# First gather stage of a graph network kernel: eight slots for gathered rows in place of four

## The reference, cut to what matters

```python
h = jnp.maximum(_layernorm(x, axis=-1), 0.0)
x_i = x[dst]
x_j = x[src]
edge_features = jnp.concatenate([x_i, x_j - x_i], axis=-1)
h = jax.nn.relu(edge_features @ W1 + b1)
edge_messages = h @ W2 + b2
out = jax.ops.segment_max(edge_messages, dst, num_segments=x.shape[0])
```

## Time and profile before

| | before |
|---|---|
| median of 3 runs | 5961.24 us (5958.34 to 5966.22) |
| span of the profiled execution, first to last instruction | 5916.2 us |
| instructions | 34006 |
| POOL busy | 3570.2 us (60%) |
| PE busy | 2544.0 us (43%) |
| DVE busy | 2042.2 us (35%) |
| ACT busy | 1398.4 us (24%) |

### The profile page before, as it was taken

How to read it: one execution, slowest core, us unless ns; L and a number is a source line. 1 busy time by engine, 2 the same in 40 slices (tenths; PEclk the granted TensorE clock), 3 DMA queues, 4 the chain that set the end, 5 groups by cost and what they waited for, 6 DMA issues and landing times. The chain is left out here.

```text
span 5916.2 us, 34006 instructions
## 1 busy us (share of the span) xinstructions
PE 2544.0 (43%) x8675; PEld 1514.2 (26%) x8675; DVE 2042.2 (35%) x2739; ACT 1398.4 (24%) x2486; POOL 3570.2 (60%) x3776
## 2 busy tenths in 40 slices
PE   2114444444444444441144444443444444457776
PEld 1012222222222222221022222222222222235555
DVE  5212222222222222224322222222222222269995
ACT  6101111111111111111111111111111111148884
POOL 5666666666666666665566666666666666631112
PEclk9986655666566666665565566566666656668887
DMA  9512222222222222222233333333333333369993
GB/s 356 161 44 66 73 70 68 72 70 70 69 70 74 66 73 71 68 72 50 53 95 91 87 97 87 98 98 87 97 88 98 88 93 93 96 211 420 422 420 130
DMA packets 351133, 696.87 MB, mean 118 GB/s; under 512 B 133445, under 2 KB 190543, under 8 KB 304247
## 3 DMA queue, kind: packets, MB, share of 16 engines
q1 hardware_dynamic: 204908, 558.27, 25.6%
q0 software_dynamic: 119328, 128.91, 10.9%
q10 hardware_dynamic: 26706, 7.50, 0.6%
HBM read 349.70 MB, written 344.74 MB: 117 GB/s over the span
## 5 line engine op out<-in xcount | busy, mean ns | idle before, releaser
L985 POOL DMA_INDIRECT pairs<-norm_table,node_sums x1664 | 1573.8, 946 | 795.7 <-issue 473.4
L711 POOL DMA_INDIRECT send_in<-send_table,node_sums x1664 | 1573.8, 946 | 773.0 <-issue 486.2
L1006 PE MATMUL ps_hid<-pairs_t,w1a 128*128 128x512 f32 x832 | 689.6, 924 | 1146.5 <-issue 667.8
L723 PE MATMUL ps_msg<-hidden,w_twice 128*128 128x512 f32 x416 | 423.0, 1119 | 1338.3 <-issue 919.3
L1095 DVE TENSOR_SCALAR hid<-ps_hid,vec 128x512 f32<-128x512 f32 x416 | 311.7, 749 | 1743.8 <-remote 989.0
L1041 ACT COPY pairs_t<-ps_pairs 128x512 f32<-128x512 f32 x416 | 244.0, 587 | 1640.1 <-DMA recv_edges<-node_sums 1100.7
L794 DVE TENSOR_TENSOR_SCAN filled<-mask,filled,ps_recv 128x512 f32<-128x512 f32 x208 | 266.2, 1280 | 879.9 <-ACT mask L757 712.4
L757 ACT COPY mask<-ps_mask 128x512 f32<-128x512 f32 x208 | 121.9, 586 | 1652.3 <-remote 894.2
L1228 DVE TENSOR_TENSOR_SCAN total<-ps_mask,total,hid 128x1024 f32<-128x1024 f32 x208 | 488.7, 2350 | 49.7 <-PE ps_mask L1178 24.8
L1006 PEld LDWEIGHTS ps_hid<-pairs_t,w1a 128*128 128x128 f32 x832 | 182.8, 273 | 1232.5 <-issue 721.1
L785 DVE TENSOR_TENSOR_SCAN maxima<-mask,maxima,ps_msg 128x512 f32<-128x512 f32 x208 | 266.2, 1280 | 631.7 <-issue 347.3
(11 more groups left out here) (174 smaller groups left out, 2952.9 us busy)
## 6 DMA issues: line engine op xcount, KB each, us to landing
hid_edges<-hid SPq DMA_DIRECT2D x104, 1024.0 KB
hid<-hid_edges SPq DMA_DIRECT2D x104, 1024.0 KB
hid_edges<-rows SPq DMA_DIRECT2D x104, 1024.0 KB
recv_edges<-node_sums SPq DMA_DIRECT2D x52, 1024.0 KB
recv_in<-recv_edges SPq DMA_DIRECT2D x208, 256.0 KB
max_edges<-max_rows SPq DMA_DIRECT2D x208, 256.0 KB
edge_in<-in_edge_attr_dram SPq DMA_DIRECT2D x415, 128.0 KB
send_in<-send_table,node_sums POOLq DMA_INDIRECT x1664
```

The lines of the kernel that those rows point to most:

```text
L711: pool.indirect_dma_start(out=send_in[:, s, j, t, :], out_offset=None, in_=send_table, in_offset=bass.IndirectOffsetOnAxis(ap=src_cols[:, ...
L723: nc.tensor.matmul(ps_msg[:, :], w2_twice[:, :], hidden[:, s % 2, :], start=True, stop=True).then_inc(msg_done, 1)
L985: pool.indirect_dma_start(out=pairs[:, s, j, 0:C], out_offset=None, in_=norm_table, in_offset=bass.IndirectOffsetOnAxis(ap=src_cols[:, k, ...
L1006: nc.tensor.matmul(ps_hid[s % 2][:, :], w1a[:, :], pairs_t[:, s % 2, :], start=True, stop=True).then_inc(multiplied, 1)
```

## The change

`send_in` gets eight slots, and each slot its own semaphore in `gathered`. POOL's step k waits until PE has turned step k-8 instead of step k-4, and PE waits for the semaphore of slot k modulo 8. `U`, by which the other buffers go, stays at four.

```diff
             U = 4
...
-            send_in = tensor(s2, "send_in", [P, U, J, 2, C])
+            DEEP = 8
+            send_in = tensor(s2, "send_in", [P, DEEP, J, 2, C])
...
-            gathered = [sem(f"gathered{i}") for i in range(U)]
+            gathered = [sem(f"gathered{i}") for i in range(DEEP)]
...
                 def gather(r, s):
                     k = r * U + s
-                    at_least_apart(pool, send_turned, k - U + 1, pool_passed)
+                    at_least_apart(pool, send_turned, k - DEEP + 1, pool_passed)
                     for t in range(2):
                         for j in range(J):
-                            pool.indirect_dma_start(out=send_in[:, s, j, t, :], out_offset=None, in_=send_table,
+                            pool.indirect_dma_start(out=send_in[:, k % DEEP, j, t, :], out_offset=None, in_=send_table,
                                                     in_offset=bass.IndirectOffsetOnAxis(ap=src_cols[:, t * HB + k, j:j + 1], axis=0)
-                                                    ).then_inc(gathered[s], 16)
+                                                    ).then_inc(gathered[k % DEEP], 16)
...
-                    at_least(pe, gathered[s], 16 * 2 * J * (r + 1))
+                    at_least(pe, gathered[k % DEEP], 16 * 2 * J * (k // DEEP + 1))
                     at_least(pe, join_done, k - 1)
                     for j in range(J):
-                        mm = nc.tensor.transpose(ps_send[s % 2][:, j::J], send_in[:, s, j, :, :].rearrange("p t c -> p (t c)"), ident[:, :])
+                        mm = nc.tensor.transpose(ps_send[s % 2][:, j::J], send_in[:, k % DEEP, j, :, :].rearrange("p t c -> p (t c)"), ident[:, :])
```

## The result

| | before | after |
|---|---|---|
| median of the runs, us | 5962.91 (5958.34 to 5966.22, 4 runs) | 5995.01 (5988.67 to 6004.24, 4 runs) |
| ratio | 1 | 1.0055, 95% interval 1.0044 to 1.0067 |
| profiled execution: span, us | 5916.2 | 5996.8 |

The account below looks back on a forecast made before the run. PE, held back by POOL's unbroken gathers, was taken as the bound. POOL ending 5.8 us earlier and PE's +30.3 at the end gave +24.5: 5916.2 + 45.0 + 24.5 = 5986 us, range 5944 to 6000 (own range 5973 to 6000).

Parts of the forecast that it names:

- Slots and semaphores cost nothing: Eight slots and semaphores add no instruction cost; POOL issues the same 1664 gathers: estimate 0.
- The middle keeps its pace: First gather stage, middle: the run-and-pause pattern shifts by four steps, pace stays 11.290 us a step, change 0.
- First wait before step 12, twelve steps of gathers against four joins: Stage's beginning: POOL first waits at step 12; at 464 us twelve steps of gathers stand against four joins.
- Its length, 9.0 us: POOL's first wait lasts 9.0 us, so step 12 starts at 473.7; bounds 4.1 and 15.5 us.
- Four more steps of PE at the end, +30.3 us: Stage's end: PE is at step 199, not 203, and does four more steps alone at 7.58 us: +30.3.
- POOL done a few us earlier: Stage's end: POOL's step 207 starts at 2675.3 against 2681.07, 5.8 us earlier.
- 45.0 us lie around the span: Profiled span 5916.2 us is 45.0 below the runs' median 5961.24; these 45.0 were taken as lying around the span.
- The reading that unbroken gathers hold PE back: First gather stage: long unbroken runs of POOL's gathers hold PE back, and a pause of POOL frees it.
- no change: Rival, chance 0.23: PE's late results have another cause, such as its own instruction count; 5961 us.
- A little faster: Rival, chance 0.10: the crawl of steps 2 and 3 belongs to the start itself; -14.8 us, 5946 us.
- Far faster: Rival, chance 0.07: POOL's pauses are the trouble and vanish; -232 us, 5729 us.
- Much slower: Rival, chance 0.05: runs of seven steps replace three, 12.9 us a step, +300 us, above 6200 us.

Follow-up runs that it names:

- the other trace of before: The unchanged kernel with four slots, profiled once more on another chip: 5981.01 us, span 5979.3 us.
- the runs without gathers: Kernel before with each step's eight gathers replaced by plain loads of other rows: 5115.67 us issued by SP, 5131.21 us by POOL.
- the gathers that nobody waits for: Kernel before with PE working on SP's plain loads, POOL issuing its 1664 gathers into tiles nobody reads: 7032.2 us (before 5954.48).

## Why the prediction was right, and where it was off

- **Slots and semaphores cost nothing**: right. Eight slots at the old distance, 0.9996.
- **The middle keeps its pace**: right. 158 joins in 1800 us in the changed and in the unchanged kernel, 157 with two and with sixteen slots. The absolute mark, 11.290 us a step, was too narrow: between the 41st and the 191st join the trace of after has 11.41, two executions of before 11.27 and 11.44. The reason given, one pattern shifted by four steps, was not tested by itself; what stays open, below, names another. The same holds for "some 70 waits": 101 after, 110 in an unchanged kernel.
- **First wait before step 12, twelve steps of gathers against four joins**: right (96 gathers, 4 joins).
- **Its length, 9.0 us**: the term that was mis-sized. It is 15.17 us, and I had the right value as the upper bound (15.5, if the wait grows with the run). In these traces it does: 5.6, 9.3, 15.2 and 26.2 us with 2, 4, 8 and 16 slots. So POOL's step 12 starts 1.7 us later than before from the stage's start, not 4 us earlier. My bound for a step held throughout, 40.6 us, was near the 42.0 that it is; with it, step 4 is turned at 478 and the wait is 13 us (478 - 464.7).
- **Four more steps of PE at the end, +30.3 us**: right. +30.5 us between the two traces, 26.6 against the other trace of before in the table.
- **POOL done a few us earlier**: not between these two traces, where its last step starts 2357.0 us after its first gather against 2336.6 before. The middle of after is slower in that execution, and so is its second stage; against the 2363.1 of the other trace of before, it is 6 us earlier.
- **The sum**: 1.7 + 30.5 + 0 for the middle = 32.2 us, and the medians differ by 32.1. I had 24.5, with -4.1 for step 12 and -1.8 that came in by 11.290 us a step, where the same trace has 11.299 from step 12 on. That the parts meet the medians within 0.1 us is partly luck: each varies by some us from trace to trace.
- **"45.0 us lie around the span"**: wrong. Each run's time is 1.9 us above its own span (5998.66 against 5996.8 in the profiled run of after). The profiled execution of before was itself shorter: 5918.1 us by this, with 5958.34 the shortest of the timed ones. On other chips the kernel before has medians of 5919 and 5925 us, so the trace may be of another chip. The forecast was not hurt, since the 24.5 us were added to the median in effect.
- **The reading that unbroken gathers hold PE back**: shown. PE at 42.0 us a step beside gathers with which it shares nothing, at 7.5 us once they are over. **That a pause frees it** was too simple. Pauses of 1.8 us free nothing, and the longer the run, the later PE comes free: POOL's last gather ended 9.4 us before the held join in before (414.27 to 423.63), 14.9 in after (470.5 to 485.45) and 26.0 with sixteen slots (578.6 to 604.55), after some 70, 120 and 230 us of gathers. Where they ran for 2303 us (to 2653), the join at 2672.07 still came 42.0 us after the one before it, and the next followed after 10.5.
- **The second gather stage as support**: weaker than it was put. Of its 5.65 us a step, four gathers alone take 5.0 by the 10.02 us for eight.

The rivals: *no change* falls with the runs without gathers (PE's own instruction count allows 7.5 us a step) and with sixteen slots. *A little faster* falls with 42.0 us, step after step, far from the stage's start. *Far faster* falls with sixteen slots, where gathers issued twelve steps earlier cost 1.36%, and with the gathers that nobody waits for, which took 2303 us and not 2085. The Trainium skill's rule (issue early, wait late: "DMA: Bandwidth & Descriptors", rules for kernel authors) did not help here: PE had waited 13.0 us for gathered rows. *Much slower* falls with the unchanged middle.

What stays open: by what path a gather holds PE back; whether it is its indirect form or its 128 single rows (no plain load of single rows was tried); and why the middle settles near 11.4 us a step, with anything from two to sixteen slots and with eight more PE instructions.

To the last question one answer fits the numbers; it was not tested: gathers, in the long run, do not go faster than one in 1.40 us. As an estimate from the run in which nobody waits for them, eight are then 11.2 us; the second gather stage has 5.65 us for four, 1.41 each. POOL issues one in 1.25 us for as long as a run is short, and what is left over after 70, 120 and 230 us of it, a share of 0.15 / 1.40, would be 7.5, 12.9 and 24.6 us, near the 9.4, 14.9 and 26.0 us above. If so, POOL's waits in the middle are time that it could not have used in any case. A run of gathers with PE at rest would tell.

## What to carry to other kernels

Before deepening a buffer, look at who is late: where the consumer is, the filler stands exactly as many steps ahead as there are slots, and every further slot only adds a step to what is left after the filler's last one (7.5 us here). Its waits are then not idle time to be won, however large their sum; the fewest slots that keep the consumer fed are best, two here (one was not tried). And a slow consumer may be slowed by the filler itself: give it the same data by another way, or run the filler for nobody, and see. The second also tells how fast the filler is without its waits: 2303 us here, against 2345 with them.

## What the runs showed of the hardware that was not expected

- While POOL issues gathers without a pause, PE gets through one weight load or product in 1.400 us: 42.0 us for a step of 30, 53.20 us for one of 38, and 42.00 us at either level of its clock. Without gathers the step of 30 takes 7.5 us.
- 3328 plain loads of 32 KB, issued by POOL with 0.3 us of idle time, and 167 GB/s in all, did nothing to PE.
- Where SP issued eight plain loads a step beside them, and POOL waited for nobody, gathers came 1.25 us apart for the first 200 us or so and 1.40 us later, as many as the loads and products that PE got through.
